# First attention: a third stack buffer, maxima spread one to a slot, shift rows sent in pieces

## The reference

```
xg = x.reshape(b, 8, c // 8, n);  xn = (xg - mean) * rsqrt(var + 1e-5) * norm_w + norm_b
qkv = einsum('oc,bcn->bon', qkv_w, xn) + qkv_b          # 8 heads, d = 16, n = 1024
attn = softmax(einsum('bhdn,bhdm->bhnm', q * scale, k * scale))
out = einsum('bhnm,bhdm->bhdn', attn, v).reshape(b, c, n)
x = einsum('oc,bcn->bon', proj_w, out) + proj_b + x
x = x + conv_block(group_norm(x))                        # reads the normed image, here called u
```

## Time and profile before

| what | us |
|---|---|
| median of 3 runs (5458.4 to 5465.98) | 5458.73 |
| the profiled execution, device time | 5458.14 |
| its span in the trace | 5456.3 |
| first shifted score of the attention to the last | 92.5 to 2026.9 |
| the 13 images between the projections of the first and the fourteenth | 273.78 to 1866.63 |
| convolution's first matmul | 2078.76 |

### The profile page before, as it was taken

One profiled execution on the slowest core, in us unless ns is written; L12 is line 12 of the kernel. 1 busy time (PEld: TensorE's weight loads), 2 busy tenths in 40 slices (PEclk: granted clock), 3 DMA queues, 4 the chain that ended last, 5 costly groups with the idle time before them and its releaser, 6 DMA issues.

```text
span 5456.3 us, 90109 instructions
## 1 busy us (share of the span) xinstructions
PE 4884.0 (90%) x29729; PEld 2693.7 (49%) x29729; DVE 3601.6 (66%) x7699; ACT 2986.6 (55%) x5452; POOL 1018.5 (19%) x1348
## 2 busy tenths in 40 slices
PE   5999999999999988868888888889899999999999
PEld 1222222232222222247777777778755555555554
DVE  6777777777777744555656656555676766766765
ACT  2666666666666663315555555556655455555552
POOL 2221122232121222112333333333200000000000
PEclk7999999999999998879999999999999999999999
DMA  2522222232222211305454545454311111111112
GB/s 85 148 78 88 71 71 81 74 94 84 71 93 72 68 45 28 72 32 154 144 163 142 164 139 165 139 156 115 111 44 48 53 44 51 50 42 51 51 46 74
DMA packets 406330, 477.63 MB, mean 88 GB/s; under 512 B 87640, under 2 KB 249648, under 8 KB 403760
## 3 DMA queue, kind: packets, MB, share of 16 engines
q1 hardware_dynamic: 372128, 424.84, 25.8%
q0 software_dynamic: 20576, 35.55, 2.4%
q10 hardware_dynamic: 13168, 11.48, 0.8%
HBM read 308.54 MB, written 145.57 MB: 83 GB/s over the span
## 4 chain that ended last, share of the span: by engine, by line
PE 34%; DVE 16%; issue 3%; DVEq 3%; ACT 2%; ACTq 0%; SPq 0%; DMA 0%
PE n_ps_f L2157 4%; PE n_ps_f L2150 4%; PE n_ps_xy L1805 3%; PE n_ps_h L1795 3%; PE n_ps_c L2197 2%; PE n_ps_h L2209 2%; PE n_ps_f L2144 2%; PE n_ps_f L1653 2%; PE n_ps_xy L2213 1%; DVE n_stats L975 1%; PE n_ps_f L999 1%; DVE n_xln L987 1%; PE n_ps_h L2213 1%; DVEq L2029 1%; DVE n_down_weights L2028 1%
## 5 line engine op out<-in xcount | busy, mean ns | idle before, releaser
L600 ACT ACTIVATE a_probs<-ps_b 128x512 f32<-128x512 f32 x2048 | 1111.0, 594 | 734.9 <-PE ps_b L696 725.1
L456 DVE TENSOR_REDUCE a_negmax<-ps_a 128x1 f32<-128x1024 f32 x1024 | 1219.7, 1221 | 309.6 <-PE ps_a L640 301.1
L696 PE MATMUL ps_b<-a_q_stack,a_k_stack 99*128 99x512 bf16 x2048 | 651.7, 391 | 56.9 <-DMA a_q_stack<-a_shift 49.3
L640 PE MATMUL ps_a<-a_k_stack,a_q_stack 96*128 96x512 bf16 x2048 | 624.9, 403 | 74.3 <-DMA a_k_stack<-split_scratch 64.4
L710 PE MATMUL ps_o<-a_probs,a_v_ones 128*32 128x256 f32 x8192 | 670.5, 400 | 0.0
L1608 ACT ACTIVATE n_hidden<-n_ps_h,n_b 128x128 f32<-128x128 f32 x1472 | 419.3, 373 | 343.6 <-PE n_ps_h L1795 342.3
L1805 PE MATMUL n_ps_xy<-n_down_weights,n_hidden 128*128 x2944 | 409.7, 284 | 80.4 <-ACT n_xy L1622 74.2
L1805 PEld LDWEIGHTS n_ps_xy<-n_down_weights,n_hidden 128*128 128x128 f32 x2944 | 368.5, 196 | 118.2 <-issue 114.6
L2094 ACT ACTIVATE n_down_weights<-n_ps_h 128x512 f32<-128x512 f32 x288 | 172.1, 598 | 428.6 <-PE n_ps_h L2209 323.0
L1795 PE MATMUL n_ps_h<-n_xy,n_up_weights 128*128 128x128 f32 x2944 | 400.9, 280 | 4.5 <-issue 2.4
L696 PEld LDWEIGHTS ps_b<-a_q_stack,a_k_stack 99*128 99x128 bf16 x2048 | 201.0, 100 | 382.1 <-ACT a_probs L600 98.8
(11 more groups left out here) (346 smaller groups left out, 7655.8 us busy)
## 6 DMA issues: line engine op xcount, KB each, us to landing
n_up_weights<-in_L_ffn_W_dram SPq DMA_DIRECT2D x368, 256.0 KB
n_up_weights<-score_scratch SPq DMA_DIRECT2D x512, 128.0 KB, 2.9
split_scratch<-a_pieces SPq DMA_DIRECT2D x180, 256.0 KB
a_q_stack<-split_scratch SPq DMA_DIRECT2D x128, 192.0 KB, 3.6
a_k_stack<-split_scratch SPq DMA_DIRECT2D x128, 192.0 KB, 4.1
rows_scratch<-n_zero SPq DMA_DIRECT2D x16, 1472.0 KB, 10.0
outs_scratch<-n_xy SPq DMA_DIRECT2D x176, 128.0 KB, 2.0
n_xg<-rows_scratch SPq DMA_DIRECT2D x80, 256.0 KB, 3.2
```

The source lines that it names most:

```text
L456: dve.tensor_reduce(negmax[:, b, t:t + 1], bank, axis=AX.X, op=ALU.max, negate=True).then_inc(ring_read, 1)
L600: act.activation(probs[:, m % PROBS, 512 * k:512 * k + 512], ps_b[:, k, :], ACT.Exp).then_inc(b_exp, 1)
L640: last = pe.matmul(bank[:, cols], q_stack[0:KS, h, 128 * t:128 * t + 128], k_stack[0:KS, h, cols], start=True, stop=True)
L696: pe.matmul(ps_b[:, k, :], k_stack[:, h, 128 * t:128 * t + 128], q_stack[:, h, 512 * k:512 * k + 512], start=True, stop=True).then_inc(b_u ...
```

## The change

- **A third stack buffer.** `STACKS = 3`; group `G i + g` uses buffer `(G i + g) % 3`. The third lies in the space of the four last images of `u_cols`. SP may load a group once the group three before it has had its last shifted scores. Group 0 of the next image is loaded right after its pieces are stored, before the shifts of the current image's group 1; group 1 of the next image after these.
- **The four last images of u** (`LATE`) go to a DRAM scratch `u_dram` instead, and the convolution phase loads them back in three parts (fills 0 and 1, fills 2 to 7, the rest), the first of which its first matmul waits for. The filter rows move to the three images before these.
- **Maxima one to a slot, four slots earlier.** Slots 0 to 27 hold the maxima 4 to 31 of the image's group 1, slots 28 to 59 those of the next image's group 0, slots 60 to 63 the first four of its group 1. The shifts are in slots 13, 29, 45 and 61. The prologue forms four more maxima.
- **Other works** move: `sums` and `norm` of the first norm to slot 2, `qk` to 6 and 8, `v` to 10, `recip` to 11; `sums` of the second norm to 33, `norm2` to 34, `turn2` to 36. `project` and `moments2` stay in 29 and 30.
- **Shift rows piece by piece.** POOL signals each of the three pieces, and SP sends each when it is there.

```diff
@@ attention_phase
+        STACKS = 3
         HELD = 3
-        rows = u_cols[:, B - HELD:B, :, :]...
+        spare = u_cols[:, B - LATE:B, :, :].rearrange("p a c h -> p (a c h)").bitcast(BF16)
+        q_spare, k_spare = (spare[0:KS + PIECES, J * N * n:J * N * (n + 1)].rearrange("p (j n) -> p j n", j=J) for n in range(2))
+        q_stacks = [q_stack[:, 0:J, :], q_stack[:, J:2 * J, :], q_spare]
+        k_stacks = [k_stack[:, 0:J, :], k_stack[:, J:2 * J, :], k_spare]
+        rows = u_cols[:, B - LATE - HELD:B - LATE, :, :]...
...
         def normed():
-            work = [(0, ("moments",)), (1, ("sums", 0)), (1, ("norm",))]
-            return work + [(4, ("qk", 0)), (6, ("qk", 1)), (9, ("v",))]
+            work = [(0, ("moments",)), (2, ("sums", 0)), (2, ("norm",))]
+            return work + [(6, ("qk", 0)), (8, ("qk", 1)), (10, ("v",))]
         def projected():
-            return [(2, ("take", 1, 0)), (4, ("take", 1, 1)), (8, ("recip",)), (29, ("project",)), (30, ("moments2",)),
-                    (31, ("sums", 1)), (32, ("norm2",)), (34, ("turn2",))]
+            return [(2, ("take", 1, 0)), (4, ("take", 1, 1)), (11, ("recip",)), (29, ("project",)), (30, ("moments2",)),
+                    (33, ("sums", 1)), (34, ("norm2",)), (36, ("turn2",))]
         def maxima(ahead, g):
-            work = [(3 + n * 26 // QUAD, ("scores", ahead, g, n)) for n in range(QUAD)]
-            return work + [(18, ("shift", ahead, g, 0)), (30, ("shift", ahead, g, 1))]
+            return [("scores", ahead, g, n) for n in range(QUAD)]
+        EARLIER = 4
+        def all_maxima(front):
+            work = [(n, w) for n, w in enumerate(maxima(0, 1)[EARLIER:])]
+            work += [(13, ("shift", 0, 1, 0)), (29, ("shift", 0, 1, 1))]
+            if front:
+                work += [(QUAD - EARLIER + n, w) for n, w in enumerate(maxima(1, 0) + maxima(1, 1)[:EARLIER])]
+                work += [(45, ("shift", 1, 0, 0)), (61, ("shift", 1, 0, 1))]
+            return work
...
             def send_shift(i, g, pair):
-                sp.wait_ge(shift_up, i * (2 * G) + 2 * g + pair + 1)
                 for p in range(PIECES):
+                    sp.wait_ge(shift_up, (i * (2 * G) + 2 * g + pair) * PIECES + p + 1)
                     sp.dma_start(...).then_inc(shift_in[pair], 16)
...
             def body(prev, i, front, back, load):
-                if back:
-                    sp.wait_ge(b_up, i * (2 * SLOTS))
-                load_stack(i, 1)
...
                 if front:
                     store_split(0, i + 1)
                     store_split(1, i + 1)
+                    load_stack(i + 1, 0)
                 send_shift(i, 1, 0)
                 send_shift(i, 1, 1)
                 if front:
-                    sp.wait_ge(b_up, i * (2 * SLOTS) + 2 * QUAD)
-                    load_stack(i + 1, 0)
+                    load_stack(i + 1, 1)
@@ conv_phase
+            for n, up in enumerate(late_in):
+                part = slice(PARTS[n], PARTS[n + 1])
+                sp.dma_start(u_cols[:, B - LATE:B, part, :]..., u_dram[:, :, part, :]...).then_inc(up, 16)
```

71 lines of the change are left out of this document (44 added, 27 removed).

## The result

The changed kernel takes 5572.33 us (median of 4 runs, 5563.99 to 5577.5), the kernel before beside it 5458.56 (5452.34 to 5465.98): ratio **1.0208**, 95% interval 1.0190 to 1.0225. That is +114 us where +29 was forecast, and outside the range of 5420 to 5530. The sign held, and so did the stalls and the slow clock behind them; one term did not.

A forecast was written before the change was run, and what follows sets the result against it. The prediction took PE to be the engine to cost, with DVE able to hold the ring. It summed 124.3 us an image against 122.5; 5458 + 25 for 14 middle images + 4 for edges gave 5487 us, range 5420 to 5530.

The forecast's parts named there:

- the term for the stacks: PE's waits for stack loads, 2.3 us an image, were to go because stacks are loaded half an image earlier.
- the walk: Slot-by-slot reckoning of PE waiting for DVE through the ring of banks: stalls of 4.9 and 6.5 us an image.
- PE's own work: PE's matmul work in an image at full clock, taken as 108.5 us.
- First norm: New PE stalls for DVE in slots 0 to 4: 0.5, 0.9 and 3.4 us, sum 4.9 an image.
- Second norm: New PE stalls for DVE in slots 29 to 38: 1.4, 0.4, 0.6, 2.1, 0.65 and 1.3, sum 6.5 us.
- Clock: PE's half clock, 7 us at each norm's stalls, costing 2.2 and 1.5 us an image.
- the third case: Rival, chance 0.20: both stall places pay the full 3.5 us for the slow clock in every image.
- Waits that go: Old waits removed: stacks 2.3, shift rows 2.9, moments 1.2, ACT 1.6; together 8.0 us an image.
- Edges: Prologue +4.7, last image about -4, convolution's first matmul +2.9, its next filters 0 to 3; taken as +4 us.
- Clearly slower: Rival, chance 0.20: half clock costs 3.5 to 4.5 us at each stall place; 127 an image, 5525 us.
- A little faster: Rival, chance 0.18: stalls come but the clock doesn't fall, or falls inside them; 120.6 an image, 5435 us.
- clearly faster: Rival, chance 0.09: DVE's chains overlap PE, half of 11.4 us shows; 116.7 to 119 an image, 5380 to 5410 us.

The follow-up runs named there:

- e1: Changed kernel with `recip` back in slot 8 instead of 11, all else of the change kept: 5477.55 us, ratio 1.0036.
- e8: Changed kernel with `recip` in slot 8 and filler matmuls ahead of slots 4 (14) and 35 (8): 5435.74 us, ratio 0.9971.
- e3: Changed kernel with needless filler matmuls on PE ahead of slot 4 (14) and slot 35 (8) in middle images: 5511.73 us, ratio 1.0099.
- e4: Changed kernel with the whole slot table of the kernel before; third buffer and shift rows by pieces stay: 5391.57 us, ratio 0.9875.
- e5: Kernel before with the shift rows sent piece by piece, nothing else: 5393.48 us, ratio 0.9893.
- e10: Kernel before with `recip` in slot 11 instead of 8, nothing else: 5460.71 us, ratio 1.0013.
- e14: Changed kernel with `recip` in slot 10 instead of 11: 5479.54 us, ratio 1.0039.
- e12: Changed kernel with SP's load of the next image put behind the stack loads: 5534.43 us, ratio 1.0137.
- e9: Changed kernel with q's six stores issued on SP ahead of the reciprocals' store and loads: 5570.39 us, ratio 1.0218.

## Why the prediction was wrong

**The step that failed** is the term for the stacks: "Stacks are loaded half an image earlier, so the 2.3 us go", with "SP runs past its new queue in time". It counted the loads ahead of the shift rows, where SP indeed has time, and not what stands ahead of the loads. `recip` from slot 8 to 11 is in the diff and in the prose on the change, and the sum has no term for it: on DVE it goes behind the v read, and on SP the store of the reciprocals is the wait behind which 4.7 MB are queued. What would have shown it is the DMA traffic of the kernel before behind the same loads (605.34); here it is from 605 to 645 us, one number for each us:

```profile
GB/s 0 131 336 188 221 209 242 326 199 205 201 219 205 201 207 199 207 201 197 205 203 207 202 53 3 0 8 0 16 0 0 0 0 0 0 0 0 0 0 0
```

The block took 23 us there, and nothing waited for its end, since SP stood for POOL's shift pieces next. With `recip` in slot 11 and the stack's first use in slot 28 there are 17 slots, 26 us at 1.54, for the way from the reciprocal to its loads (2.05, 641.27 to 643.32), 23 to 24 of transfers, and the stack's own first load (3.2, 667.50 to 670.66): 2 to 3 us were missing. The miss is the difference between the changed kernel and e1, 93 us, 5.8 in each period: 3.3 of waiting at slot 28 and 0.7 at the shift (L668, behind `recip` on DVE). The other 1.8 I put down to the clock, which is 0.94 there and 0.96 in e1, with PE busy 2.3 us an image longer. Another 9.2 us lie ahead of the first projection (285.30 against 276.14). (The two profiled executions differ by 94.1; their last 9 us, behind the convolution's start, are scatter as above.)

**What held**, by the prediction's steps:

- *Forecast without that term.* 124.3 an image and 5487 us; e1, which is the change without the late `recip`, has 124.1 and 5477.6. That it meets the period within 0.2 is in part luck. In e8, at full clock, waits (5.2 an image) and fillers (4.9) stand where the walk has 11.4, and the other 110.8 us of its period stand against 108.5 + 0.7; the clock was 3.2, not 3.7. PE's own work was taken about 1.6 too low, and stalls and clock about 1.8 too high.
- *First norm*, 4.9 (its own terms, 0.5, 0.9 and 3.4, give 4.8): 0.21, 0.75 and 3.58, 4.5. *Second norm*, 6.5: 1.27 + 0.48 + 0.34 + 1.76 = 3.9. The 0.65 and 1.3 behind slot 35 are not there, since PE at half clock gives DVE time to catch up. They are there as 0.51 and 1.18 where the clock stays full (e8, and e3), so the walk had them; the prediction named the overlap and counted it on the clock's side only.
- *Clock*, 3.7: 3.2 by e8 against e1, and 3.8 by e3 against the changed kernel (0.4 of it stack waits). In the changed kernel the granted clock was 0.50 to 0.74 in the 3.5 us behind each of the 39 waits of slots 4, 28 and 35. The rule that the Trainium skill gives (TensorE: Matmul & The Clock Gate, "HAM oscillation — how this bites in real kernels") holds there, in that the slow clock returned at every one of these places in every image; in e1 it stayed away behind 2 of the 13 waits at slot 35. Its price was less than the full 3.5 us a place that the third case took, 1.6 to 1.9.
- *Waits that go.* The shift rows' 2.9 and the moments' 1.2 went. The prediction's sum by differences had 13.6 us of old waits and clock against 15.8 of new, which is +2.2 and not quite the +1.8 of its sum of an image. The balance held (e1 has +1.5), but the runs split it otherwise: the two good parts take 4.4 off the period (e4) and the table, without the late `recip`, puts 5.9 on (e1 against e4). A removed wait was worth more in clock than in wait (e5), and less beside the other than alone, which the sum didn't have.
- *Edges*, +4: the last two images -7.1 (forecast -4, bound -6, for the last alone), from the last projection to the convolution's first matmul +2.0 (forecast +2.9, bounds 1.5 and 5). The first image's +4.7 can't be told from the noise of its start, which is 273.8 in one run of nearly the same code and 276.4 in another (e10).

**The rivals.** "Clearly slower" had the right side and a wrong cause: the clock at the two chains didn't cost more, the stack came late. It was also priced too low by its own terms: 3.5 to 4.5 at each of two places on 120.6 is 127.6 to 129.6 an image, 5533 to 5561 us, and not 127 and 5525, so the range ended short of its own slow case. The sentence that would have led there stands at the end of the forecast, "if they still came late, it would add 2 us an image to the slow side"; it was given no chance of its own and no place in the range, and 2 was too low, since the wait was longer than the old one and brings its half clock with it. "A little faster" and "clearly faster" needed the chains to be hidden or the clock to stand, and neither was so.

**Settled and open.** Settled by e1, e10 and e14: the loss of 93 us comes with the late reciprocal, and only in the changed kernel, which wants the stack in slot 28. No run has the late reciprocal with the third buffer and the old table, which would tell the early use from the early loads. e12 supports that the transfers in front set the delay. Open: whether SP's order alone could repair it (e9), and why the stores move at the rate below. The 0.7 us at the shift is given to `recip` by its place on DVE and its near absence in e1, e14 and e8 (0.3 us, once in each), not by a run of its own.

## What to carry to other kernels

When a step moves, follow every wait on every queue behind it, down to the last transfer that is queued there, and set its bytes over the measured rate against the time of the first use; a small operation three slots later can hold megabytes. The gain of a removed wait is what the next constraint leaves of it: two waits that stand over the same chain on another engine give one gain, not two. Much of that gain can be clock: compare PE's busy time for the same matmuls, not only its waits. And split a change before taking or dropping it whole, since here two parts bring 65 us and the third costs 179, 93 of them by one number.
